# Level sums of three attention layers: which operand stands still in the PE array, and in which half of it

## The reference, cut to what matters

```python
def _gat_conv(x, src, dst, W, a_src, a_dst, b, n_nodes):
    h = x @ W
    alpha_s = h @ a_src
    alpha_d = h @ a_dst
    e = alpha_s[src] + alpha_d[dst]
    e = jnp.where(e > 0, e, NEG_SLOPE * e)
    m = jax.ops.segment_max(e, dst, num_segments=n_nodes)
    ex = jnp.exp(e - m[dst])
    s = jax.ops.segment_sum(ex, dst, num_segments=n_nodes)
    alpha = ex / (s[dst] + 1e-16)
    return jax.ops.segment_sum(alpha[:, None] * h[src], dst, num_segments=n_nodes) + b
```

## Time and profile before

| what | value |
|---|---|
| median of 3 runs | 2073.58 us (2072.67 to 2073.6) |
| profiled execution | 2075.87 us, span 2074.0 us |
| attention stage | from about 1276 to 1925 us of the span |
| granted TensorE clock, mean | 0.941 of full speed |
| level sums, all layers | 1875 matmuls and as many weight loads |

### The profile page before, as it was taken

One profiled execution on the slowest core, in us unless ns is written; L12 is line 12 of the kernel. 1 busy time (PEld: TensorE's weight loads), 2 busy tenths in 40 slices (PEclk: granted clock), 3 DMA queues, 4 the chain that ended last, 5 costly groups with the idle time before them and its releaser, 6 DMA issues. The chain is left out here.

```text
span 2074.0 us, 36733 instructions
## 1 busy us (share of the span) xinstructions
PE 1681.0 (81%) x9771; PEld 854.7 (41%) x9772; DVE 1490.4 (72%) x3987; ACT 1158.5 (56%) x2276; POOL 1115.0 (54%) x983
## 2 busy tenths in 40 slices
PE   1777777684799999999899895799979997999675
PEld 0222222352344444444444444545344534443444
DVE  5999999435577777777777674678857896788554
ACT  5777777312344444444444442489858985898211
POOL 1000000001777777777777772399959994999200
PEclk9999999897899999999999996799989998999877
DMA  7000000101111111111111114000000000000000
GB/s 183 0 0 0 0 0 0 77 1 54 31 41 34 39 35 34 39 35 39 34 34 39 34 29 121 5 1 1 1 1 1 1 1 1 1 1 8 9 1 16
DMA packets 29632, 50.72 MB, mean 24 GB/s; under 512 B 12820, under 2 KB 13826, under 8 KB 29054
## 3 DMA queue, kind: packets, MB, share of 16 engines
q1 hardware_dynamic: 11890, 31.59, 5.1%
q0 software_dynamic: 17664, 18.12, 5.1%
HBM read 36.58 MB, written 7.39 MB: 21 GB/s over the span
## 5 line engine op out<-in xcount | busy, mean ns | idle before, releaser
L809 POOL DMA_INDIRECT adj<-h_table,l_idx x544 | 570.0, 1048 | 166.4 <-issue 157.8
L1541 POOL TENSOR_TENSOR gat_ring<-gat_ring,adj 125x750 f32<-125x750 f32 (+2 forms) x375 | 507.7, 1378 | 91.4 <-ACT gat_ring L1595 85.8
L999 DVE TENSOR_SCALAR adj<-adj,node_key 125x1024 f16<-125x1024 f16 x825 | 380.2, 503 | 203.9 <-PE psum L944 180.9
L944 PE MATMUL psum<-adj,x_sb 125*128 125x512 f16 x1650 | 403.7, 389 | 1.3 <-DVE adj L999 1.3
L1448 DVE SCALAR_TENSOR_TENSOR gat_ring<-x_sb,gat_node,psum 125x750 f32<-125x750 f32 (+2 forms) x375 | 315.8, 859 | 89.3 <-PE psum L1669 48.8
L387 PE MATMUL psum<-col_hot,src_hot 128*128 128x500 bf16 x808 | 205.6, 376 | 114.9 <-DVE src_hot L316 93.5
L872 ACT ACTIVATE l_z<-psum 128x320 f32<-128x320 f32 x204 | 89.2, 437 | 343.4 <-PE psum L923 343.3
L1666 PE MATMUL psum<-gat_ring,gat_hx 125*65 125x500 f32 (+1 forms) x500 | 250.1, 585 | 17.9 <-POOL gat_ring L1541 16.2
L721 POOL MEMSET l_aggT<- 64x3146 f32 x1 | 2.7, 2713 | 478.1 <-POOLq L1730 478.1
L313 DVE TENSOR_SCALAR col_hot<-iota_h,c_tab 128x500 bf16<-128x500 f16 x808 | 227.4, 345 | 25.1 <-PE psum L387 21.1
L1592 ACT ACTIVATE gat_ring<-gat_ring,gat_node 125x750 f32<-125x750 f32 (+2 forms) x267 | 217.7, 815 | 41.9 <-DVE gat_ring L1448 38.8
(11 more groups left out here) (241 smaller groups left out, 2080.5 us busy)
## 6 DMA issues: line engine op xcount, KB each, us to landing
adj<-h_table,l_idx POOLq DMA_INDIRECT x544, 2.6
adj<-key_table SPq DMA_DIRECT2D x33, 250.0 KB
adj<-adj SPq DMA_DIRECT2D x3, 1662.5 KB
adj_saved<-adj SPq DMA_DIRECT2D x1, 3840.3 KB
adj<-adj_saved SPq DMA_DIRECT2D x5, 688.2 KB
x_sb<-in_x SPq DMA_DIRECT2D x1, 781.2 KB
x_saved<-x_sb SPq DMA_DIRECT2D x1, 781.2 KB
out<-x_sb SPq DMA_DIRECT2D x5, 156.2 KB
```

Source lines behind the costliest of these rows:

```text
L809: pool.indirect_dma_start(out=to[:, t, :], out_offset=None, in_=table[:, :], in_offset=bass.IndirectOffsetOnAxis(ap=index[:, t:t + 1], axi ...
L944: last = pe.matmul(psum[:, PAIR[half] + t, :], h_parts[:, k, :], select[0:P, k % SELECTS, t * GE:(t + 1) * GE], start=(k == 0), stop=(k == ...
L999: v.tensor_scalar(select[0:P, k % SELECTS, :], keys, node_key[:, k:k + 1], None, ALU.is_equal).then_inc(s_sel, 1)
L1541: pool.tensor_tensor(slot, slot, adj[:, k, cols(c)], ALU.mult).then_inc(s["weight_ready"], 1)
```

## The change

The levels become the stationary operand (125 x 64) and the adjacency the moving one (125 x 500 and 125 x 250 columns). Source tiles are taken in pairs: even k writes PSUM partitions 0 to 63, odd k partitions 64 to 127, of the two banks 4 and 5. A group is 13 steps (`PAIRS`, the last with one k), each of two or four matmuls. The sums now stand with levels on the partitions and destinations along them. VectorE clips 128 rows of them at once with limits for each partition, by which the 64th and the 128th row (the degrees) pass unchanged. `turn_levels` multiplies each tile of 125 columns as stationary operand by `picks` (128 x 4), and that gives four numbers for a destination: the levels' sum and the degree of each half. `node_step` 1 takes the larger of the two level sums, and the degree is the sum of the other two.

Chunk 1's 13 pairs stand behind steps 0 to 12 of chunk 0; from then on a coming chunk's pairs are spread over the steps from 20 of one chunk to 12 of the next. The turn stands behind step 15 on TensorE, the clip behind k = 17 on VectorE.

```diff
-    PROJECT_AT, ABSORB_AT, SUMMED_AT, NODE_AT = 6, 11, 17, 20
+    LEVELS_IN = 4
+    PROJECT_AT, ABSORB_AT, SUMMED_AT, CLIP_AT, TURN_AT, NODE_AT = 6, 11, 13, 17, 15, 20
...
             def degrees_in(g):
-                sums = level_sums_of(g)[:, :, WINDOWS]
-                v.tensor_scalar(deg[:, tiles_of(g)], sums, -1.0, None, ALU.add).then_inc(s["degrees_read"], 1)
+                mine = counts[:, :, 0:GCHUNK[g]]
+                v.tensor_copy(mine, turned_levels(g)[:, :, 2:4].rearrange("p t j -> p j t")).then_inc(s["degrees_read"], 1)
+                dve.wait_ge(s["degrees_read"], 2 * g + 1)
+                v.scalar_tensor_tensor(deg[:, tiles_of(g)], mine[:, 0, :].bitcast(FP32), -1.0, mine[:, 1, :].bitcast(FP32),
+                                       ALU.add, ALU.add).then_inc(s["degrees_read"], 1)
...
                 if i == 0:
                     dve.wait_ge(s["levels_summed"], g + 1)
+                if i == 1:
+                    dve.wait_ge(s["levels_turned"], g + 1)
...
-                    op = v.tensor_scalar(mine, level_sums_of(g)[:, :, 0:WINDOWS].bitcast(I32), LOW_CODE, HIGH_CODE, ALU.max, ALU.min)
+                    op = v.tensor_scalar(by_tile(clipped[:, 0:width(g % GC)]),
+                                         pair(LEVELS_IN, 128)[:, 0:GCHUNK[g % GC], 0:P].bitcast(I32),
+                                         limits[:, 0:1], limits[:, 1:2], ALU.max, ALU.min)
                 elif i == 1:
-                    op = v.tensor_reduce(m, mine, AX.X, ALU.add)
+                    op = v.tensor_reduce(m, turned_levels(g)[:, :, 0:2], AX.X, ALU.max)
...
+            link = Chain(dve, s["shift_chain"])
+            dve.wait_ge(s["constants"], 4)
+            for half in range(2):
+                last_row = ident[:, half * LEVELS + WINDOWS:half * LEVELS + LEVELS]
+                link(v.tensor_tensor(picks[:, half:half + 1], picks[:, half:half + 1], last_row, ALU.subtract))
+                link(v.tensor_copy(picks[:, 2 + half:3 + half], last_row))
+            link(v.tensor_tensor(limits[:, 0:1], picks[:, 0:1], picks[:, 1:2], ALU.add))
+            link(v.tensor_scalar(limits[:, 1:2], limits[:, 0:1], HIGH_CODE - COUNT_CODE, COUNT_CODE, ALU.mult, ALU.add))
+            link(v.tensor_scalar(limits[:, 0:1], limits[:, 0:1], LOW_CODE, None, ALU.mult))
...
-                            for i in {NODE_AT - 1: (0,), NODE_AT: (1, 2), NODE_AT + 1: (3, 4, 5)}.get(k, ()):
+                            for i in {CLIP_AT: (0,), NODE_AT: (1, 2), NODE_AT + 1: (3, 4, 5)}.get(k, ()):
...
+            pool.memset(picks[:, :], 0.0).then_inc(s["constants"], 1)
+            pool.wait_ge(s["constants"], 2)
+            for half in range(2):
+                pool.memset(picks[half * LEVELS:(half + 1) * LEVELS, half:half + 1], 1.0).then_inc(s["constants"], 1)
+            pool.wait_ge(s["constants"], 4)
...
-            def level_sum(g, i):
+            def level_sums(g, i):
                 c = g % GC
-                t, k = divmod(i, NT)
                 if i == 0:
                     pe.wait_ge(s["levels_ready"], g // GC + 1)
-                    if g >= 2:
-                        pe.wait_ge(s["node_rows"], 6 * (g - 1))
-                    if 2 <= g < GC + 2:
-                        pe.wait_ge(s["degrees_read"], min(g - 1, GC))
-                at = (GSTART[c] + t) * P
-                op = pe.matmul(level_sums_of(g, 128)[:, t, :], b["adj_all"][0:P, k, at:at + 128], levels[:, k, :],
-                               start=(k == 0), stop=(k == NT - 1), skip_group_check=True)
-                if i == GCHUNK[c] * NT - 1:
-                    op.then_inc(s["levels_summed"], 1)
+                    if g > 0:
+                        pe.wait_ge(s["node_rows"], 6 * (g - 1) + 2)
+                        pe.wait_ge(s["degrees_read"], 2 * min(g, GC) - 1)
+                near = min(GCHUNK[c], 4)
+                for part in [slice(0, near)] + [slice(near, GCHUNK[c])] * (GCHUNK[c] > near):
+                    for k in range(2 * i, min(2 * i + 2, NT)):
+                        at = slice((GSTART[c] + part.start) * P, (GSTART[c] + part.stop) * P)
+                        last = pe.matmul(pair(LEVELS_IN, LEVELS, k % 2 * LEVELS)[:, part, 0:P], levels[:, k, :],
+                                         by_tile(adj[:, k, at]), start=(k < 2), stop=(k >= NT - 2), skip_group_check=True)
+                if i == PAIRS - 1:
+                    last.then_inc(s["levels_summed"], 1)
+
+            def turn_levels(g):
+                pe.wait_ge(s["node_rows"], 6 * g + 1)
+                for t in range(GCHUNK[g % GC]):
+                    last = pe.matmul(turned_levels(g)[:, t, :], clipped[:, t * P:(t + 1) * P], picks[:, :],
+                                     start=True, stop=True, skip_group_check=True)
+                last.then_inc(s["levels_turned"], 1)
...
-                        n = c * NT + k + 1
-                        if n <= SUMMED_AT:
-                            target = -(-GCHUNK[1] * NT * n // SUMMED_AT)
-                        else:
-                            whole, part = divmod(n - SUMMED_AT, NT)
-                            target = NT * sum(GCHUNK[1:2 + whole]) + part * sum(GCHUNK[2 + whole:3 + whole])
+                        if k < SUMMED_AT:
+                            ahead = NT - NODE_AT if c > 0 else 0
+                            target = PAIRS * c + PAIRS * (ahead + k + 1) // (ahead + SUMMED_AT)
+                        elif k >= NODE_AT:
+                            target = PAIRS * (c + 1) + PAIRS * (k - NODE_AT + 1) // (NT - NODE_AT + SUMMED_AT)
                         while taken < min(target, len(coming)):
-                            level_sum(*coming[taken])
+                            level_sums(*coming[taken])
                             taken += 1
+                        if c + 1 < GC and k == TURN_AT:
+                            turn_levels(g + 1)
```

More of the change, by code:

```diff
@@ L61 @@
 MARGIN_BITS = 0.05
+COUNT_CODE = float((1 << 31) - 128)
+PAIRS = -(-NT // 2)
 MATS = ["L0_W1l", "L0_W1r", "L0_W2l", "L0_W2r", "G_W1", "G_W2", "G_W3", "S_neigh1", "S_self1", "S_neigh2", "S_self2"]
@@ L1098, in gnn @@
             ring = sb("gat_ring", [P, RING, GWIDE], FP32, scope)
-            hT = sb("gat_hT", [D + 1, 2, CW], FP32, scope)
+            hT_all = sb("gat_hT", [128, 2 * GWIDE], FP32, scope)
+            hT, clipped = hT_all[0:D + 1, 0:2 * CW].rearrange("p (a b) -> p a b", a=2), hT_all[:, GWIDE:2 * GWIDE]
             wx = sb("gat_weights", [D + 1, 3, D + 3], FP32, scope)
@@ L1103, in gnn @@
             levels = sb("gat_levels", [P, NT, LEVELS], BF16, scope)
-            starts_i = sb("gat_window_starts_i", [P, WINDOWS], I32, scope)
+            picks = sb("gat_level_picks", [128, 4], FP32, scope)
+            limits = sb("gat_level_limits", [128, 2], FP32, scope)
+            counts = sb("gat_degree_bits", [P, 2, max(GCHUNK)], I32, scope)
+            starts_i = hT_all[0:P, 2 * CW:2 * CW + WINDOWS].bitcast(I32)
             starts = sb("gat_window_starts", [P, WINDOWS], FP32, scope)
@@ L1109, in gnn @@
                 inv_deg=inv_deg, adj=adj, psum=psum, ident=ident, x_sb=x_sb, x_flat=x_flat, aggT=aggT, vecs=vecs, deg=deg, stat=stat, ring=ring,
-                hT=hT, asd=asd, node=node, rr=rr, ext=ext, wx=wx, levels=levels, starts_i=starts_i, starts=starts, adj_all=adj_all, over_features=over_features, feats=(hx, o_all),
+                hT=hT, asd=asd, node=node, rr=rr, ext=ext, wx=wx, levels=levels, starts_i=starts_i, starts=starts, clipped=clipped, picks=picks, limits=limits, counts=counts, over_features=over_features, feats=(hx, o_all),
                 x_saved=x_saved, adj_saved=adj_saved, vecs_in=vecs_in[:, 2 * D:],
@@ L1238, in attention @@
         "adj", "psum", "ident", "x_sb", "x_flat", "aggT", "vecs", "deg", "stat", "ring", "hT", "asd", "node", "rr", "ext", "wx"))
-    levels, starts_i, starts = b["levels"], b["starts_i"], b["starts"]
+    levels, starts_i, starts, clipped, picks, limits, counts = (b[k] for k in (
+        "levels", "starts_i", "starts", "clipped", "picks", "limits", "counts"))
     codes = levels[:, :, 0:WINDOWS].bitcast(mybir.dt.int16)
@@ L1263, in attention @@
              "self_loops", "w_chain", "w_columns", "w_rows", "constants", "transposed", "transpose_copied", "first_projected",
-             "first_read", "shift_chain", "extremes", "extremes_all", "starts", "levels_ready", "levels_summed", "node_rows", "row1_in_psum",
+             "first_read", "shift_chain", "extremes", "extremes_all", "starts", "levels_ready", "levels_summed", "levels_turned", "node_rows", "row1_in_psum",
              "row2_in_psum", "row2_copied", "exponent_raw", "exponent_ready", "exponent_bounded", "exp_ready", "weight_ready", "product_done",
@@ L1283, in bounded_to, with pair, turned_levels @@
         return sum(bounded_by_dve(i // NT % GC, i % NT) for i in range(g * NT + k + 1))
[L1285 to L1289, removed]
+    def pair(bank, rows=P, first=0):
```

(16 more changed lines are left out.)

6 lines of the change are left out of this document (2 added, 4 removed).

## The result

| | median | range | runs |
|---|---|---|---|
| before | 2073.12 us | 2071.78 to 2073.6 | 4 |
| after | 2095.05 us | 2094.18 to 2097.23 | 4 |

The changed kernel is slower by 21.9 us: ratio 1.0108, interval 1.0091 to 1.0126. The forecast was 2105 us, + 31. The profiled execution took 2095.2 us, with a span of 2093.1.

The account below looks back on a forecast made before the run. In attention, TensorE bounds chunk 0; GpSimd and ScalarE hold 6-tile chunks at 42.5 us, TensorE 1 to 2 below. Per layer 3.5 + 2 x 2.5 + 0 + 1.7 = 10.2, three layers + 31: 2105 us, range 2079 to 2162.

Parts of the forecast that it names:

- (a): TensorE's sums: the two halves of a 6-tile pair stream side by side, 0.31 us a pair against 0.35 before.
- the halves take turns: Rival, chance 0.25: the two halves of a pair don't overlap on TensorE, 0.31 us more each; 2155 us.
- (b): TensorE, a pair between two products: each change of width costs some 0.1 us, so 0.2 us a pair.
- changes of width are hidden: Rival, chance 0.19: TensorE's width changes cost nothing and the halves overlap; 4.1 us a layer, 2086 us.
- (c): TensorE's turn of the sums: 25 more matmuls a layer, 1.3 us for 6 tiles; wait for the clip costed at nothing.
- (d): VectorE in a chunk: clip 0.99 us against 0.55, reduction 0.2 against 0.54, sum about 0; early small operations hidden, 0.
- lengths of chunks 1 and 2: Chunks 1 and 2 of each layer: TensorE's 44.4 us plus waits, 44.4 to 46.3, taken as 45.2, + 2.5 each.
- Chunk 0: First chunk of each layer, 3 tiles: TensorE's work 28.9 us against 25.1, taken as + 3.5 us.
- Chunk 3: Fourth chunk of each layer: TensorE's 40.4 us stays under GpSimd's 42.5, so 0, bounds 0 and 0.5.
- sign of being wrong: Length of the 6-tile chunks: the forecast is wrong if they stay at 42.7 us or pass 47.
- The *start: Start of each layer, first sums to rows: clip, turns, reduction, width change and a semaphore step, sum + 1.7 us.
- the rows come earlier: Rival, chance 0.11: earlier clip and shorter reduction cut waits before row 2 of 12 chunks, up to 11 us; 2068 us.

Follow-up runs that it names:

- e1: The changed kernel with source tiles reordered, all even k first, then all odd k, so neighbouring pair matmuls use the same half; ratio to before 1.0269.
- e6: The kernel before plus one tiny matmul of 64 stationary columns behind every second step of chunks 0 to 3; ratio to before 1.0064.
- e7: The kernel before plus the same tiny matmuls as e6, but with 128 stationary columns, so no change of width; ratio to before 1.0010.
- e2: The changed kernel with pairs issued two at a time, 7 bursts a chunk instead of 13; ratio to before 1.0044.
- e3: The changed kernel with every turn made twice, same data and same place; ratio to before 1.0201.
- e9: The kernel before plus idle matmuls ahead of each layer's first sums and 12 more behind row 1; ratio to before 0.9945.

## Why the prediction was right, and where its sizes were off

The direction, the mechanism and the range held; + 31 was forecast and + 21.9 measured. That it came no farther off is in part luck, since the misses have both signs: by the stage, the starts cost 2.6 us more than forecast, chunks 3 and 4 together 1.1 more, chunk 0 2.0 less, chunks 1 and 2 together 8.0 less. By its own steps:

(a) *Stream of the sums*, 0.31 us a pair: right. The trace has both halves 3 ns apart, and e1 prices the overlap at 0.31 to 0.32 us. The rival "the halves take turns" is refuted.

(b) *In and out of halves*, 0.20 us: right, 0.19 by e6 against e7. The rival "changes of width are hidden" falls by these and by e2. For the chosen pair cost of 0.51 us, chunk 0's trace has 0.56: a step with a pair starts every 1.22 us (1549.37, 1550.59, 1551.81) and a product takes 0.66 of it. That the 6-tile chunks did not come out longer for it is owed to terms counted a little high: rows 1 and 2 take 2.6 us for 2.9, and a product with nothing behind it 1.26 for 1.29.

(c) *Turning*, 1.3 us for 6 tiles and on TensorE's path: right, by step 15 (2.49 - 1.26 = 1.23 us) and by e3. No turn within a chunk waited for its clip, as assumed.

(d) *VectorE*: the clip takes 1.05 us for the 0.99 assumed, the reduction 0.16. These are the groups by shape of the changed kernel:

```profile
L1437 DVE TENSOR_SCALAR gat_hT<-psum,gat_level_limits 128x750 f32<-128x750 int32 x9 | 9.5, 1052 | 0.0
L1441 DVE TENSOR_REDUCE gat_node<-psum 125x6 f32<-125x12 f32 x9 | 1.5, 163 | 0.3
```

No 6-tile clip waited for the sums. From the stage's first transpose to layer 0's first sum it is 36.2 us against 36.0, so the prelude's additions were hidden, as said.

The *terms that were mis-sized* are the lengths of chunks 1 and 2, + 2.5 each in every layer, 15 in all; measured are 7.0. TensorE's work in them, 44.4 us, was counted well: chunk 1 lasts 43.8 to 44.4 us and chunk 2 43.6 to 44.8. What failed is the choice of 45.2 between 44.4 and 46.3: I had added TensorE's present waits at a chunk's end on top, and they did not stay. These are chunks 1 and 2 of layer 0, cut at TensorE's first product, of the kernel before, the changed one and e6:

```profile
1353.65:1397.15 43.50, 41.63 (x281) 21.89 (x281) 32.74 (x43) 38.46 (x48) 41.00 (x26) 1.00 0.00 1
1397.15:1439.62 42.47, 41.21 (x276) 21.80 (x273) 34.95 (x43) 37.83 (x47) 39.38 (x26) 1.00 0.00 1
1353.65:1398.06 44.41, 43.98 (x192) 19.00 (x192) 33.73 (x45) 39.35 (x48) 41.58 (x27) 1.00 0.00 1
1398.06:1442.83 44.77, 44.30 (x194) 19.66 (x193) 34.53 (x44) 38.89 (x46) 38.90 (x25) 1.00 0.00 1
1481.16:1525.52 44.36, 43.58 (x293) 23.55 (x293) 34.93 (x43) 38.91 (x48) 41.32 (x26) 1.00 0.01 1
1525.52:1569.70 44.18, 43.54 (x284) 23.70 (x283) 33.97 (x43) 37.93 (x47) 39.30 (x25) 1.00 0.00 1
```

TensorE was idle for 1.9 and 1.3 us before and for 0.4 and 0.5 us after. An engine with more work waits less; but there may be a second cause, shifts that are ready earlier for the rows. These are the rows over the whole stage, in the same order of kernels (idle time before them behind the last bar):

```profile
L1645 PE MATMUL psum<-ident,gat_shifts 125*125 125x125 f32 x300 | 40.4, 284 | 20.6 <-DVE gat_shifts L1435 14.3 <-DVE gat_ring L1448 6.3
L1680 PE MATMUL psum<-ident,gat_shifts 125*125 125x125 f32 x300 | 42.8, 296 | 8.5 <-DVE gat_shifts L1449 4.4 <-DVE gat_ring L1462 4.0
L1645 PE MATMUL psum<-ident,gat_shifts 125*125 125x125 f32 x300 | 43.7, 299 | 16.2 <-DVE gat_shifts L1435 12.1 <-DVE gat_ring L1448 4.1
```

The waits at the rows are 12.1 us shorter, 1.9 of them at the three starts (3 x 1.74 against 3 x 1.11), 10.2 within the chunks. e6 has the old clip and reduction and chunks 1 and 2 about as long as the changed kernel's, and lost 4.4 us of these waits. The rest fits the earlier clip and the shorter reduction, but no run moves the clip alone, so how the 12.1 us divide isn't shown. Also the base of 42.7 was ScalarE's cut; at TensorE's, chunk 1 had 43.4 already. Chunk 0 was forecast at + 3.5 and is + 2.8: there a wait of 0.9 to 1.0 us at row 2 is gone as well. Chunk 3, forecast at 0, is + 0.1. In ScalarE's cut, in which the signs were written down, chunk 1 stayed at 42.5 us, where 42.7 was named as a sign of being wrong; the sign was bound to the wrong cut.

The *start* was under-sized: + 1.7 a layer, measured + 2.0, + 3.3, + 2.4. I took the clock as given, and in layer 1 the changed kernel kept it at 1.2 GHz through turn and rows (+ 1.3 us in the rows alone). From the clip's end to the reduction, with the turn between, it is 1.5 us for the 1.2 assumed. The 0.2 us that the sum allows for one more semaphore step has no row behind it and no run measures it alone.

The rival "the rows come earlier" needed a pair below 0.31 us with its excursion; it has 0.56, and as a forecast of the total it falls. Its mechanism does not: it would have cut the waits at the rows of 12 chunks by up to 11 us, they are 10.2 us shorter, and the sum of the forecast had put that at nothing. (The 17.1 us that it names from the earlier trace rows are those of the weight loads; the matmuls themselves waited 14.3 us for the shifts.)

## What to carry to other kernels

Count an engine by the distance of its starts. Where it is to become the bound, don't add its present waits unasked: look at what each waits for, and whether the change moves that too. Array halves pay in streamed columns but each trip to them from full-width work costs 0.19 us here, so they want bursts, and an operand turned afterwards is work on the same engine. Here TensorE idles for 8 and 3 us ahead of a stretch that it bounds, and idle matmuls in both gaps were worth 0.55%, 9.1 us of the stage. By my estimate that is more than the change of operands could have been: at most 0.5 us from the stream for each of the 15 groups, 7.5 us. Look at a variant's granted clock before its stage is compared: e3 and e6 differed from their partners by it too.

## What the hardware showed beyond that

Two 64-column matmuls of 500 columns start 3 ns apart and take 0.23 us together until the next two. By the Trainium skill ("TensorE: Matmul & The Clock Gate", Part 3) matmuls in different column positions span one duration plus some 4 ns for each further one; the trace agrees.

A full-width matmul of 64 columns takes 29 to 30 ns from start to start with a new weight load each (75 sums in 2.36 us in e9, the last one's 0.19 us included). Streaming 750 columns in two halves at once is hardly faster than that: 0.31 us for twelve sums' 0.35, by which the change could have won 0.5 us a chunk.

The granted clock was at 0.50 twice in the start of layer 1 of the kernel before: for most of the 8 us in which TensorE waits for VectorE's levels and on into the sums, and again for 3.4 us from the first product on, behind the wait of 3 us. In e1 it was at 1.00 by the turn of layer 1, behind 5.38 us of sums; in the changed kernel, with 4.30 us of sums, it was at 0.50 until the third step, and behind layer 2's 3.82 us of sums it was at 1.00 for the turn alone. Each is one execution, and what decides between them isn't shown.
